# An even tile's queries in one product: scores and value sums of a local attention inside a two-layer block

## The reference

```
bq = q.reshape(b, h, w, WINDOW, d) * QK_SCALE
bk, bv = (look_around(bk), look_around(bv))       # window before and own window: 128 keys
sim = jnp.einsum('bhwid,bhwjd->bhwij', bq, bk)
mask = (i < j) | (i > j + WINDOW) | (j == -1)
sim = jnp.where(mask, -jnp.finfo(sim.dtype).max, sim)
attn = jax.nn.softmax(sim, axis=-1)
out = jnp.einsum('bhwij,bhwjd->bhwid', attn, bv)
```

## Time and profile before

| | |
|---|---|
| median of 3 executions | 962.86 us (961.32, 962.86, 966.73) |
| the profiled execution, its own time | 961.04 us |
| its span, first to last instruction | 959.2 us |
| mean granted TensorE clock | 0.969 of full |
| PE busy | 790.5 us, 82% of the span, 7311 products |
| DVE, ACT, POOL busy | 666.8, 660.4, 543.3 us |

### The profile page before, as it was taken

How to read it: one execution, slowest core, us unless ns; L and a number is a source line. 1 busy time by engine, 2 the same in 40 slices (tenths; PEclk the granted TensorE clock), 3 DMA queues, 4 the chain that set the end, 5 groups by cost and what they waited for, 6 DMA issues and landing times.

```text
span 959.2 us, 19697 instructions
## 1 busy us (share of the span) xinstructions
PE 790.5 (82%) x7311; PEld 562.6 (59%) x7311; DVE 666.8 (70%) x1575; ACT 660.4 (69%) x1545; POOL 543.3 (57%) x326
## 2 busy tenths in 40 slices
PE   5867888888789888878879879988879888878884
PEld 5745656556466655555556655656556566556552
DVE  4667875867787866676786877576787766686732
ACT  2345757778776857868775866767776877768682
POOL 3176741858685544595766743293967762575800
PEclk9988899999999999999999989999999999999997
DMA  6000000000000000000000000000000000000000
GB/s 207 1 12 12 2 2 1 1 2 2 1 2 18 6 1 12 13 1 2 1 1 1 23 1 12 7 7 1 2 1 1 12 2 12 2 1 2 1 1 23
DMA packets 12278, 9.89 MB, mean 10 GB/s; under 512 B 1040, under 2 KB 11288, under 8 KB 12184
## 3 DMA queue, kind: packets, MB, share of 16 engines
q1 hardware_dynamic: 12184, 8.64, 2.9%
HBM read 6.54 MB, written 2.10 MB: 9 GB/s over the span
## 4 chain that ended last, share of the span: by engine, by line
PE 38%; DVE 22%; ACT 15%; issue 12%; POOL 12%; DMA 0%; POOLq 0%; SPq 0%; ACTq 0%; DVEq 0%
PE pair L734 7%; POOL roots L1556 5%; ACT probs L1034 5%; PE dense L888 4%; PE pair L816 3%; PE mixed L780 3%; DVE space L1480 3%; POOL qk L1604 3%; DVE qk L1279 3%; PE dense L969 2%; DVE q_norm L1485 2%; PE dense L852 2%; PE dense L853 2%; PE dense L854 2%; PE dense L734 2%
## 5 line engine op out<-in xcount | busy, mean ns | idle before, releaser
L1604 POOL TENSOR_TENSOR qk<-space 128x512 f32<-128x512 f32 x128 | 176.9, 1387 | 29.9 <-DVE q_norm L1485 26.7
L1556 POOL TENSOR_TENSOR roots<-powers,minus_half 128x32 f32<-128x32 f32 (+1 forms) x33 | 175.0, 5302 | 16.0 <-DVE powers L1493 14.9
L1034 ACT ACTIVATE probs<-pair,neg_max 128x128 f32<-128x128 f32 x512 | 139.2, 397 | 14.6 <-DVE neg_max L1301 14.2
L969 PE MATMUL dense<-wq_hi,h_hi 128*128 128x512 f32 x192 | 91.5, 476 | 49.9 <-DVE space L1480 24.5
L1601 POOL TENSOR_TENSOR space<-space,tables 128x512 f32<-128x512 f32 x64 | 86.6, 1353 | 55.8 <-ACT space L1161 55.7
L1480 DVE TENSOR_TENSOR space<-dense,tables 128x512 f32<-128x512 f32 x128 | 87.5, 683 | 37.0 <-ACT space L1161 36.7
L1301 DVE TENSOR_REDUCE neg_max<-pair 128x4 f32<-128x512 f32 x128 | 81.8, 683 | 39.4 <-PE pair L816 39.3
L1157 ACT ACTIVATE squares<-dense 128x512 f32<-128x512 f32 x128 | 79.0, 617 | 32.4 <-PE dense L971 31.9
L734 PE MATMUL pair<-eye_s,probs 128*128 128x128 f32 x512 | 77.1, 286 | 18.8 <-ACT probs L1034 18.7
L1485 DVE TENSOR_REDUCE q_norm<-squares 128x8 f32<-128x512 f32 x128 | 86.4, 675 | 0.0
L1279 DVE TENSOR_TENSOR qk<-qk,roots 128x2048 f32<-128x2048 f32 x32 | 78.6, 2456 | 8.1 <-POOL roots L1556 8.1
(11 more groups left out here) (210 smaller groups left out, 1861.7 us busy)
## 6 DMA issues: line engine op xcount, KB each, us to landing
x_in<-n_L_attn_embeddings_dram SPq DMA_DIRECT2D x8, 256.0 KB, 2.9
out_dram<-hn SPq DMA_DIRECT2D x8, 256.0 KB, 2.3
qk<-in_L_ffn_wqkv_dram SPq DMA_DIRECT2D x1, 1536.0 KB, 9.1
qk<-in_L_ffn_w_dram SPq DMA_DIRECT2D x1, 682.0 KB, 10.4
wo_s<-in_L_ffn_wo_dram SPq DMA_DIRECT2D x2, 256.0 KB
o_t<-in_L_wmod_dram SPq DMA_DIRECT2D x1, 384.0 KB, 4.4
band_s<-const_band_dram SPq DMA_DIRECT2D x1, 256.0 KB, 4.9
probs<-const_rotary_dram SPq DMA_DIRECT2D x1, 256.0 KB, 9.3
```

Of the source, the lines that this page charges most:

```text
L969: pe.matmul(to[:, :], h_hi[:, rows], wq_hi[:, layer, cols], start=True, stop=False)
L1034: last = act.activation(probs[:, ring, hh, :], banks[m][:, hh * P:(hh + 1) * P], ACT.Exp, bias=neg_max[:, ring, hh:hh + 1], scale=1.0)
L1556: return pool.tensor_tensor(to, of, minus_half[0:of.shape[0], 0:of.shape[-1]], ALU.pow)
L1604: pool.tensor_tensor(qk[s][:, t, m * INNER:(m + 1) * INNER], turned_c[:, t % 2, m, :], turned_s[:, t % 2, m, :], ALU.add).then_inc(added, 1)
```

## The change

On the even tile the two windows are no longer taken apart. For the scores of each hh and m one product has all 128 queries as weights (64 partitions, 128 columns) and all 128 keys as moving operand; window 0 now also multiplies with the keys of window 1, where the mask holds -1e30. For the mix of each hh and m one product has all 128 columns of `probs_t` as weights and the same 65 columns of `v`. The odd tile is as before, written without the cases of the even one. No other engine's code, no semaphore and no order is changed.

```diff
--- before.py
+++ after.py
@@ -803,18 +803,21 @@
                         pe.matmul(banks[m][:, :], eye_h[:, :], mask_h[:, t % 2, :, :], start=True, stop=False,
                                   skip_group_check=True)
                     for hh in range(4):
+                        if t % 2 == 0:
+                            for m in range(2):
+                                rows = slice(DH * m, DH * (m + 1))
+                                last = pe.matmul(banks[m][:, hh * P:(hh + 1) * P], q_t[rows, 0, hh, :], k_t[rows, hh, P:2 * P],
+                                                 start=False, stop=True, skip_group_check=True)
+                                if hh == 3:
+                                    last.then_inc(scored, 1)
+                            continue
                         for w in range(2):
                             for m in range(2):
                                 rows = slice(DH * m, DH * (m + 1))
                                 keys = k_t[rows, hh, :]
-                                if t % 2:
-                                    keys = keys[:, 0:P] if w else \
-                                        keys.rearrange("p (a b) -> p a b", b=WIN)[:, 0:4:3, :]
-                                else:
-                                    keys = keys[:, P:2 * P] if w else keys[:, P:P + WIN]
-                                n = WIN if (t % 2 == 0 and w == 0) else P
-                                last = pe.matmul(banks[m][w * WIN:(w + 1) * WIN, hh * P:hh * P + n],
-                                                 q_t[rows, t % 2, hh, w * WIN:(w + 1) * WIN], keys,
+                                keys = keys[:, 0:P] if w else keys.rearrange("p (a b) -> p a b", b=WIN)[:, 0:4:3, :]
+                                last = pe.matmul(banks[m][w * WIN:(w + 1) * WIN, hh * P:(hh + 1) * P],
+                                                 q_t[rows, 1, hh, w * WIN:(w + 1) * WIN], keys,
                                                  start=False, stop=True, skip_group_check=True)
                                 if hh == 3 and w == 1:
                                     last.then_inc(scored, 1)
@@ -837,10 +840,14 @@
                             pe.wait_ge(*read_at(i if slot else i - 1, (slot - 1) % 4, (PROJ, "tile", t, 2)))
                         for hh in range(4):
                             head = 2 * hh + m
+                            if t % 2 == 0:
+                                last = pe.matmul((mixed, banks[1])[m][:, hh * VW:(hh + 1) * VW],
+                                                 probs_t[:, m, hh, :], v[s][:, t, head, :], start=True, stop=True)
+                                continue
                             for w in range(2):
-                                values = v_cross[s][:, t // 2, head, :] if (t % 2 and w == 0) else v[s][:, t, head, :]
+                                values = v[s][:, t, head, :] if w else v_cross[s][:, t // 2, head, :]
                                 last = pe.matmul((mixed, banks[1])[m][w * WIN:(w + 1) * WIN, hh * VW:(hh + 1) * VW],
-                                                 probs_t[:, 2 * (t % 2) + m, hh, w * WIN:(w + 1) * WIN], values,
+                                                 probs_t[:, 2 + m, hh, w * WIN:(w + 1) * WIN], values,
                                                  start=True, stop=True)
                         last.then_inc(mixed_full, 1)
                 elif what == "out":
```

## The result

The changed kernel takes 972.58 us in the median of 7 executions (970.7 to 974.97), the kernel before 962.86 (7 executions now, 959.34 to 967.37). The ratio is 1.0106, 95% interval 1.0072 to 1.0141: slower by 9.7 us, against 7 forecast on the median (962.9 to 970). The profiled execution took 970.78 us, its span is 969.0.

A forecast was written before the change was run, and what follows sets the result against it. PE was taken as the most loaded engine (82% of the span, 38% of the chain), not the bound everywhere. Terms 4.0 + 1.0 + 2.0 = 7.0 us on 961.04 made 968.0, on the median 970 us; eight-in-ten range 961 to 983.

The forecast's parts named there:

- The partner cost nothing, the load doubles: Even mix on PE: the removed second-window products ran free beside the first; 128-column loads set 0.107 us a product.
- Shape changes are worth something, not enough: Around the even mix: steps of 0.33 us become 0.24, yet a mix is 0.45 longer, 0.65 from a wait.
- The scores: no change but the first load: Even tile's scores on PE: lanes run side by side, only the first load adds 0.05 us; 19 on the chain, 1.0.
- Seven mixes on the chain, 4.0 us: Even mixes on the profiled chain: four from a wait add 2.6 us, three from busy neighbours 1.35, together 4.0.
- A sixth of the other 12 us, 2.0: The 25 even mixes off the chain put 12.0 us on PE; a sixth, 2.0, was let through into the time.
- The sum: Whole kernel: 4.0 for mixes on the chain, 1.0 for scores, 2.0 for the other mixes, 7.0 us slower.

The follow-up runs named there:

- experiment 5: Changed kernel with each even mix product moving 120 columns of values in place of 65, except head 7: 970.58 us, ratio 1.0064.
- experiment 6: Kernel before, with each half of the even mix reordered, all heads of window 0 and then all of window 1: 962.92 us, ratio 0.9992.
- experiment 1: Kernel before with only the even tile's scores taken by one product, the mix as before: 963.53 us, ratio 1.0029.
- experiment 3: Kernel before with the mix merged only at the seven even tiles whose mix lay on its chain: 965.97 us, ratio 1.0046.

## Why the prediction was right

- *The partner cost nothing, the load doubles.* Right. 0.104 to 0.109 us a product against 0.107 taken; experiment 5 shows that the moving columns do not set it, and experiment 6 (by its timeline, not by its time) that two column halves side by side are what was lost.
- *Shape changes are worth something, not enough.* Right: 0.33 became 0.24 ahead of the mix. The product behind it still starts its follower after 0.31, where I had 0.24; before, the first product behind a wait, at 453.89, has the same 0.31, so I take it that its load is not hidden. With that a mix is 0.51 longer and not 0.45, from a wait up to 0.73 and not 0.65. On PE 24 x 0.51 + 8 x 0.73 = 18.1 us against 16.0 forecast; with the 1.8 of the scores 19.9, and the page shows 21.0. The two mixes at 1.2 GHz, 1.4 and 2.1 us longer than before, can account for the rest.
- *The scores: no change but the first load.* Right in kind, +0.06 for 0.05. Worth 2.3 us by experiment 1, for 1.0 in the sum; the interval of that run holds both.
- *Seven mixes on the chain, 4.0 us.* Right: 4.1 at equal clock by experiment 3, good to 0.8; the measured prices (three times 0.51, four times up to 0.73) would make it 4.5. The chain of one profiled execution did tell which tiles count.
- *A sixth of the other 12 us, 2.0.* At equal clock sized too small, 3.4, a quarter of what these mixes are longer; by the ratio alone, -0.3 to +5.1 us, 2.0 is not excluded. It was the term without a row, a guess that came out near. The chain of after shows why it can't be nil: five more even mixes are on it than before, two of them at 1.2 GHz. A path that is nearly as long as the chain takes over as soon as its own steps grow.
- *The sum.* 4.0 + 1.0 + 2.0 = 7.0 forecast; 4.1 + 2.3 + 3.4 = 9.8 by the parts, 8.4 and 9.4 by the two measurements of the whole at equal clock, 9.7 by the medians. The terms that were off were all off the same way, too small, so no error made good for another.
- *What the sum had nothing for* is the granted clock, 0.0033 lower than before in the first measurement, some 2 us of the difference by the yardstick; the 1.2 GHz around 727.71 is a part of it that the profiles show. That the change caused it is not shown: with the 120 columns, same order and same loads, the clock was 0.9680.

## What to carry to other kernels

Before two narrow products are made one wide one, look at what they do at the same time: products on different column halves of the array start within 0.01 us of each other in this trace (454.42 and 454.42 in experiment 6), so the second is free, while with 128 weight columns in float32 a product starts every 0.107 us whether 65 or 120 columns are moved. Fewer instructions are no gain by themselves; what counts is the pace of the slower of load and product. And where a kernel's execution times scatter more than the effect, list the clock of each execution beside its time: at equal clock parts of a change of 4.1 and 3.4 us added up to the whole's 7.6, where the plain means did not.

## What the runs showed that I had not expected

- Products on the two column halves keep their own pace and do not start in the program's order: a product of the second half started at 454.31, ahead of one of the first half at 454.36 that stands before it in the program (experiment 6).
- The mean granted clock of a kernel varies from execution to execution by 0.014, and the time goes with it: 6.2 us for 0.01. A reordering that costs PE 0.40 us a tile showed no loss in its time; it ran at a clock of 0.9717 and not 0.9662, which by the yardstick is worth 3.4 us.
- A change of shape (128 by 64 columns to 128 by 128 or back) costs 0.09 us between starts (0.33 and not 0.24 ahead of the mix), and the instruction behind the first one of the new shape starts late too: L970 0.33 behind L969 and not 0.23.
